# The last stages of a seven-block layer stack on one core: X kept in a reflected channel basis, trees routed from X, and the residual of the recurrence added by VectorE

## What is computed

```
x = x + _L1_attn_a_ref(_layernorm(x), ...)   # attention in segments of 64 tokens
x = x + _L1_ffn_ref(_layernorm(x), ...)      # soft decision tree, call 0
x = x + _L1_attn_b_ref(_layernorm(x), ...)   # linear recurrence (LRU)
x = x + _L1_ffn_ref(_layernorm(x), ...)      # the same tree, call 1

# tree:   gate = sigmoid(x @ Wq.T @ routers.T)              255 inner nodes
#         leaf_prob = product of gates along 8 levels        256 leaves
#         ret = leaf_prob @ leaf_values @ Wout_w.T + Wout_b
# LRU:    r, k, v = split(x @ W_rkv + b);  r = sigmoid(r);  k = exp(k)
#         u1 = scan(k * v), u2 = scan(k)   (decay lam per channel)
#         out = (u1 + g*k*v) / (u2 + g*k + 1e-6) * r  @ W_o + b_o
```

## Time and profile before

| what | value |
|---|---|
| time, median of 3 runs | 1137.93 us (1135.59 to 1144.2) |
| the profiled execution | 1128.02 us, span 1126.2 us |
| PE busy | 1003.1 us, 89% |
| DVE busy | 845.2 us, 75% |
| ACT busy | 748.8 us, 66% |
| POOL busy | 355.0 us, 32% |

### The profile page before, as it was taken

One profiled execution on the slowest core, in us unless ns is written; L12 is line 12 of the kernel. 1 busy time (PEld: TensorE's weight loads), 2 busy tenths in 40 slices (PEclk: granted clock), 3 DMA queues, 4 the chain that ended last, 5 costly groups with the idle time before them and its releaser, 6 DMA issues.

```text
span 1126.2 us, 20922 instructions
## 1 busy us (share of the span) xinstructions
PE 1003.1 (89%) x7682; PEld 622.6 (55%) x7682; DVE 845.2 (75%) x1518; ACT 748.8 (66%) x1235; POOL 355.0 (32%) x457
## 2 busy tenths in 40 slices
PE   7888899688867999899998999889898888898987
PEld 3333544387754444677653444676676775553355
DVE  4998887666654777777755776899999994768866
ACT  6895566345455447456777458687988776768885
POOL 1100057445553112000000114688878773000000
PEclk9999999899998999899999999799999998999999
DMA  7900055466641000000000000000000000000002
GB/s 189 294 0 1 1 150 160 145 200 212 220 145 66 1 0 11 2 2 2 1 2 1 0 1 10 1 3 2 3 2 3 16 3 10 1 1 1 0 1 76
DMA packets 42814, 54.53 MB, mean 48 GB/s; under 512 B 6251, under 2 KB 29372, under 8 KB 42716
## 3 DMA queue, kind: packets, MB, share of 16 engines
q1 hardware_dynamic: 38096, 42.75, 12.9%
q0 software_dynamic: 4288, 10.46, 2.5%
q10 hardware_dynamic: 332, 0.01, 0.0%
HBM read 22.11 MB, written 20.93 MB: 38 GB/s over the span
## 4 chain that ended last, share of the span: by engine, by line
PE 49%; DVE 22%; ACT 15%; issue 9%; POOL 2%; DMA 2%; SPq 0%; ACTq 0%; DVEq 0%
PE psum L88 4%; PE psum L1305 4%; PE psum L1277 3%; PE psum L954 3%; DVE arena L2510 3%; PE psum L1981 3%; DVE N L2519 3%; PE psum L1719 2%; DVE arena L2509 2%; PE psum L905 2%; PE psum L106 2%; ACT ln_std L115 2%; ACT ln_std L117 2%; PE psum L2326 2%; PE psum L918 2%
## 5 line engine op out<-in xcount | busy, mean ns | idle before, releaser
L2336 PE MATMUL psum<-ident,N 128*128 128x128 f32 x512 | 73.2, 288 | 18.4 <-POOL N L2479 17.8
L2425 ACT ACTIVATE N<-N 128x1024 f32<-128x1024 f32 x64 | 67.7, 1059 | 31.7 <-DVE N L2519 30.8
L2326 PEld LDWEIGHTS psum<-arena 32*128 32x128 f32 x1024 | 64.9, 194 | 25.7 <-issue 11.6
L88 PE MATMUL psum<-X,center 128*128 128x512 f32 x128 | 69.4, 631 | 10.6 <-DVE X L1062 4.2
L2326 PE MATMUL psum<-arena 32*128 32x128 f32 x1024 | 77.2, 293 | 1.6 <-ACT arena L2403 1.4
L768 POOL DMA_INDIRECT out_rows<-mixed,out_index x62 | 60.3, 972 | 57.1 <-DVE arena L844 32.0
L95 ACT ACTIVATE ln_sq<-psum 128x512 f32<-128x512 f32 x72 | 42.5, 591 | 52.2 <-PE psum L88 52.1
L2421 ACT ACTIVATE arena<-psum 128x1024 f32<-128x1024 f32 x64 | 65.7, 1026 | 16.9 <-PE psum L2336 16.7
L106 PE MATMUL psum<-ln_sq,mean 128*128 128x512 f32 x144 | 74.3, 607 | 2.1 <-ACT arena L151 1.1
L2336 PEld LDWEIGHTS psum<-ident,N 128*128 128x128 f32 x512 | 57.6, 146 | 28.1 <-POOL N L2479 22.9
L2479 POOL TENSOR_TENSOR N<-N,arena 128x512 f32<-128x512 f32 x64 | 67.8, 1059 | 0.0
(11 more groups left out here) (399 smaller groups left out, 2694.9 us busy)
## 6 DMA issues: line engine op xcount, KB each, us to landing
arena<-weights SPq DMA_DIRECT2D x31, 320.0 KB, 2.6
slot_rows<-zeros SPq DMA_DIRECT2D x1, 8060.0 KB, 26.6
arena<-slot_rows SPq DMA_DIRECT2D x31, 260.0 KB, 3.2
arena<-tw_rows SPq DMA_DIRECT2D x16, 256.0 KB, 3.6
arena<-out_rows SPq DMA_DIRECT2D x6, 512.0 KB, 5.0
out_dram<-arena SPq DMA_DIRECT2D x8, 256.0 KB, 2.8
arena<-in_L_attn_a_x_dram SPq DMA_DIRECT2D x3, 512.0 KB, 6.7
weights<-in_L_attn_a_eWk_dram SPq DMA_DIRECT2D x1, 1024.0 KB, 5.8
```

Source lines behind the costliest of these rows:

```text
L88: self.nc.tensor.matmul(k.bank[c % W][:], k.center[:], self.src(c), start=True, stop=True).then_inc(k.ln_centered, 1)
L2326: op = nc.tensor.matmul(scored[half][:, e * P:(e + 1) * P], k.sg_Q[b % 2][at, seg, 2 * j:2 * j + 2, :].rearrange("p h n -> p (h n)"), k.sg ...
L2336: op = nc.tensor.transpose(turned_to[:, e * P:(e + 1) * P], pr[n % 4][:, e * P:(e + 1) * P], k.ident[:])
L2425: nc.scalar.activation(pr[n % 4], pr[n % 4], ACT.Exp).then_inc(k.sg_exp, 1)
```

## The change

The reflection `k.house` is a symmetric orthogonal 128x128 matrix whose first row and column are 1/sqrt(128). In the basis that it makes, channel 0 holds the mean (times sqrt(128)), so that centring is only leaving channel 0 out.

- The norm before the segments (`TurningNorm`) multiplies by the reflection in place of the centring matrix, and DVE also copies the result back over X. From there on X stays reflected. All weights that read X or Y are multiplied by the reflection with row 0 cleared (`house_in`), and all that write to X by the reflection. This is done on PE and the weights are copied out of PSUM by DVE (for the segments' weights, in the norm) or by ACT (for the tree and the LRU, in iterations 52, 55, 56, 59 and 63 of the segments).
- The norms before both trees are gone. The trees route from X itself. Each token's 1/deviation is computed per token as a column (`RowMoments`: ACT squares a chunk, PE makes 4 products with one moving column, and ACT makes three small passes) and enters the sigmoids as their scale. So a chunk's gates are 8 sigmoids, 4 of 128x127 and 4 of 128x255, where there were 2 of 128x1024. For tree 0 these run inside the segments, for tree 1 at the LRU's end.
- The norm before the LRU (`TurnedNorm`) has no centring product. ACT squares X and DVE multiplies X.
- In the LRU the identity products are gone, and DVE adds X and the bias in the 8 instructions that write X. ACT's 8 such passes are gone.
- A tree's last level writes only the right children (512 numbers in place of 1024 per partition). The leaf values are differences for that half.
- The end turns X back with 4 products by the reflection per chunk, where there were 4 transposes.
- GpSimd builds the constants in the earlier `favor` block, and the LRU's weights are loaded with the tree's.

```diff
+class TurningNorm(Norm):
...
+        self.nc.tensor.matmul(k.bank[c % W][:], k.house, self.src(c), start=True, stop=True).then_inc(k.ln_centered, 1)
...
+    def scale(self, dve, c):
+        nc, k = self.nc, self.k
+        dve.wait_ge(k.ln_centered, self.centered0 + c + 1)
+        nc.vector.tensor_copy(self.src(c), k.bank[c % W][:]).then_inc(k.x_housed, 1)
+        dve.wait_ge(k.ln_rstd, self.n0 + c + 1)
+        nc.vector.tensor_tensor(self.dst(c), k.bank[c % W][:], k.ln_std[:, c % W, :], ALU.mult).then_inc(k.ln_out, 1)
+class TurnedNorm(TurningNorm):
...
+        self.nc.scalar.activation(self.k.ln_sq[:, c % W, :], self.src(c), ACT.Square).then_inc(self.k.ln_squared, 1)
...
+        nc.vector.tensor_tensor(self.dst(c), self.src(c), k.ln_std[:, c % W, :], ALU.mult).then_inc(k.ln_out, 1)
+class RowMoments:
...
+    def square(self, act, c):
+        k = self.k
+        if c >= 4:
+            act.wait_ge(k.tm_var, self.summed(c - 4))
+        self.nc.scalar.activation(self.squares[c % 4], k.X[:, c * CH:(c + 1) * CH], ACT.Square).then_inc(k.tm_sq, 1)
+
+    def sum(self, pe, c, to):
+        k = self.k
+        pe.wait_ge(k.tm_sq, self.summed(c))
+        for t in range(4):
+            op = self.nc.tensor.matmul(to[:, t:t + 1], self.squares[c % 4][:, t * P:(t + 1) * P], k.house_mean[:, 0:1], start=True, stop=True)
+        op.then_inc(k.tm_var, 1)
+
+    def deviation(self, act, first, end, source):
+        k, nc = self.k, self.nc
+        at, minus = (v[:, 4 * first:4 * end] for v in (self.rstd, self.minus))
+        k.tm_done += 1
+        act.wait_ge(k.tm_var, max(self.summed(c) for c in range(first, end)))
+        nc.scalar.activation(at, source, ACT.Ln, bias=k.eps[:, 0:1]).then_inc(k.tm_log, 1)
+        act.wait_ge(k.tm_log, k.tm_done)
+        nc.scalar.activation(at, at, ACT.Exp, scale=-0.5).then_inc(k.tm_rstd, 1)
+        act.wait_ge(k.tm_rstd, 2 * k.tm_done - 1)
...
-                nc.tensor.matmul(out_to[c][:], k.ident[:], k.X[:, at(b, c)], start=True, stop=False)
             if b == B - 2:
-                pe.wait_ge(k.lr_r, 2 * B)
+                pe.wait_ge(k.lr_k, 2 * B - 1)
+                pe.wait_ge(k.lr_kv, 2 * B - 1)
                 for c in range(4):
-                    pe.wait_ge(*(((k.lr_kv, 2 * B - 1), (k.lr_kv, 2 * B))[c < 2]))
-                    after.center(pe, c)
-                for c in range(2):
-                    after.variance(pe, c)
+                    moments.sum(pe, c, moment_at(c))
+            if b == B - 1:
+                for c in range(4, 6):
+                    moments.sum(pe, c, moment_at(c))
+                pe.wait_ge(k.lr_k, 2 * B)
+                pe.wait_ge(k.lr_kv, 2 * B)
+                tree_route(nc, k, pe, 1, 0)
             for c in range(2):
                 pe.wait_ge(k.lr_x, b + 1 if b + 1 < B else b + 1 + c)
-                nc.tensor.matmul(out_to[c][:], W_o, R[:, at(b, c)], start=False, stop=True).then_inc(k.lr_out, 1)
+                nc.tensor.matmul(out_to[c][:], W_o, R[:, at(b, c)], start=True, stop=True).then_inc(k.lr_out, 1)
 
         def project(b):
             for c in range(2):
...
-        def add(b):
+        def squares(b):
             for c in range(2):
-                act.wait_ge(k.lr_out, 2 * b + c + 1)
-                nc.scalar.activation(k.X[:, at(b, c)], out_to[c][:], ACT.Identity, bias=k.vec("lru_bo")).then_inc(k.lr_added, 1)
+                act.wait_ge(k.lr_added, 2 * b + c + 1)
+                moments.square(act, 2 * b + c)
 
...
-            if b == B - 1:
-                for c in range(4):
-                    after.square(act, c)
-                for c in range(2):
-                    after.deviation(act, c)
-            if b >= 1:
-                add(b - 1)
+            if b >= 2:
+                squares(b - 2)
+        squares(B - 2)
+        moments.deviation(act, 0, 4, k.bank[2][:, 0:16])
         over(B - 1)
-        add(B - 1)
+        moments.deviation(act, 4, 6, k.bank[3][:, 16:24])
+        squares(B - 1)
 
     @block.vector
...
+        def add(b):
+            for c in range(2):
+                dve.wait_ge(k.lr_out, 2 * b + c + 1)
+                nc.vector.scalar_tensor_tensor(k.X[:, at(b, c)], out_to[c][:], k.housed("lru_bo"), k.X[:, at(b, c)], ALU.add, ALU.add).then_inc(k.lr_added, 1)
...
             denominator(b)
+            if b >= 1:
+                add(b - 1)
             numerator(b)
         quotient(B - 1)
-
...
+def tree_route(nc, k, pe, call, n):
+    ready = (k.sg_x, k.lr_added)[call]
+    if call == 0 and n == 0:
+        pe.wait_ge(k.tw_copied, 7)
+    if n >= 2:
+        pe.wait_ge(k.tr_g, call * NCH + n - 1)
+    pe.wait_ge(ready, n + 1)
+    for t in range(4):
+        op = nc.tensor.matmul(tree_nodes(k, n)[:, t, 0:2 * P - 1], k.X[:, n * CH + t * P:n * CH + (t + 1) * P], k.gates[:, 0:2 * P - 1], start=True, stop=True)
+    op.then_inc(k.tr_z, 1)
...
-        op = nc.tensor.transpose(to[:, t, :], k.X[:, q * CH + t * P:q * CH + (t + 1) * P], k.ident[:])
+        op = nc.tensor.matmul(to[:, t, :], k.X[:, q * CH + t * P:q * CH + (t + 1) * P], k.house, start=True, stop=True)
...
+        for c in late:
+            moments.sum(pe, c, k.bank[2][:, 4 * c:4 * c + 4])
+        if call == 0:
+            pe.wait_ge(k.sg_ov, B * L // CH)
+            pe.wait_ge(k.sg_x, NCH)
+        else:
+            pe.wait_ge(k.lr_added, NCH)
+        tree_route(nc, k, pe, call, 1)
...
-            for s in range(2):
-                op = nc.scalar.activation(gates[n % 2][:, :, :, s], nodes[n % 2], ACT.Sigmoid, scale=(-1.0, 1.0)[s])
+            for t in range(TI):
+                at = slice(n * TI + t, n * TI + t + 1)
+                nc.scalar.activation(gates[n % 2][:, t, 0:P - 1, 0], nodes[n % 2][:, t, 0:P - 1], ACT.Sigmoid, scale=moments.minus[:, at])
+                op = nc.scalar.activation(gates[n % 2][:, t, 0:2 * P - 1, 1], nodes[n % 2][:, t, 0:2 * P - 1], ACT.Sigmoid, scale=moments.rstd[:, at])
...
+                if level == DEPTH - 1:
+                    nc.vector.tensor_tensor(lp[n % 2][1][:, :, 0:m], src, gates[n % 2][:, :, m - 1:2 * m - 1, 1], ALU.mult).then_inc(k.tr_lp, 1)
+                    continue
...
+    MOMENT = {25: 1, 28: 0, 41: 3, 44: 2, 57: 5, 60: 4, N + 1: 6}
+    SQUARE = {23: 1, 26: 0, 39: 3, 42: 2, 55: 5, 58: 4, N: 6}
+    WEIGHTS = {52: 0, 55: 1, 56: 2, 59: 3, 63: 4}
...
+            if n in MOMENT:
+                moment(n)
+            if n in WEIGHTS:
+                weights(n)
-            if n in (N + 2, N + 3):
+            if n == N + 3:
                 pe.wait_ge(k.sg_arg, N)
-                after.center(pe, n - N - 2)
+                tree_route(nc, k, pe, 0, 0)
...
+            if n in MOMENT:
+                moments.deviation(act, MOMENT[n], MOMENT[n] + 1, other[:, 0:4])
+            if n in WEIGHTS:
+                keep_tree_weights(nc, k, act, WEIGHTS[n], other)
+            if n in SQUARE:
+                act.wait_ge(k.sg_x, SQUARE[n] + 1)
+                moments.square(act, SQUARE[n])
+        act.wait_ge(k.sg_x, TURNS)
+        moments.square(act, TURNS - 1)
```

303 lines of the change are left out of this document (187 added, 116 removed).

## The result

The changed kernel is slower, not faster: median 1148.28 us (1139.25 to 1159.73, 20 runs) against 1138.28 (1131.03 to 1154.0, 20 runs) of the kernel before, ratio 1.0064, 95% interval 1.0041 to 1.0088. By the ratio that is +7.3 us, small (under the 1% of my forecast's bound) but clear of no change, where I forecast -10.9. The ratio compares fast runs alone (four runs of the changed kernel, at 1157 us and more, were in a slower state of the chip), while the medians take in all runs and so lie 10.0 us apart. The profiled execution has a span of 1148.2 us.

The account below looks back on a forecast made before the run. No engine is full overall; DVE is nearly full in segments and LRU, PE bounds a settled tree. 0.5+3-12.6-3.5-3.5+5.2 = -10.9, put on the median 1137.93, gave 1127.0 us; range 1119 to 1136.

Parts of the forecast that it names:

- the 1% of my forecast's bound: Whole kernel: about 1% (11.4 us) is what a measurement can tell from no change.
- Norm ahead, +0.5: Norm before the segments: ACT sets the pace, most added copies and products fit; +0.5 us (0 to 2).
- Insertions in the segments, +3: Sums and weight products added in the segments: most fit free PE and ACT time; +3 us (0 to 8).
- rival "slower": Segments: every insertion stalls as PE and ACT wait on bank 7; 22 us in place of 3, 1146; chance 0.05.
- Last output product to gate 0, -12.6: Segments' end to tree 0: short deviation work and table load replace the norm; -12.6 us (-13.5 to -11).
- Tree 0 and norm, -3.5: Tree 0 and the norm behind it: start +1.0, end -4.5; together -3.5 us (-5 to -1.5).
- the slow stretch that I had priced: Tree start: PE idles during gate 0, one 1.7 us route takes double length, of which 0.35 us shows.
- the rival of ACT as a tree's bound: Trees: ACT's gate and copy take 4.5 us per chunk, above PE's 4.32; total 1133; chance 0.12.
- LRU, -3.5: LRU: DVE's additions cost +2.8, the end gives -6.4, removed identity products worth nothing; -3.5 us (-5 to -1).
- PE's clock stays low: Thinned norm, LRU's end and both tree starts run at a low PE clock; +6 us, 1133; chance 0.10.
- Tree 1 and end, +5.2: Tree 1 and final turns: start +1.0, turn 6 +0.75, two-pass turns back +3.5; together +5.2 us (+4 to +8).
- my three signs of being wrong: Segments lose under 1 or over 8 us; tree turns over 4.5 apart; LRU's granted clock well below 0.96.

Follow-up runs that it names:

- e7_filler: Changed kernel with sums moved to iterations 31 and 47, plus the LRU's eight identity products back on PE, results unused: LRU 56.1 us, ratio 0.9912 to the kernel before.
- experiment 9: Changed kernel with sums moved from iterations 28 and 44 to 31 and 47, final turns as transposes, leaving out the reflection back: ratio 0.9916 to the kernel before.
- experiment 2: Changed kernel with the sums of chunks 0 and 2 moved from iterations 28 and 44 to 31 and 47: ratio 0.9901 to the kernel before.
- experiment 3: Changed kernel with two chunks' sums in one place (iterations 31, 47, 60) and one deviation for both: ratio 1.0063 to the kernel before, segments 248.0 us.

## Why the prediction was wrong

**Norm ahead, +0.5.** No run shows it or contradicts it; the spread of 701 to 720 us of the first exp buries it.

**Insertions in the segments, +3: this is the step that failed.** It went by free time per iteration ("PE has about 0.6 us free in each and ACT 0.8") and not by the place. 5.8 us is what the same work costs in good places, inside my 0 to 8. In iterations 28 and 44 the sums stand between a query projection and ACT's second read of it, and cost 13.9 us in iterations 29, 30, 45 and 46 (10.6 by the wait alone, with the slow clock behind it). Of the rest of the 21, some 5.4 us in iterations 26 to 28 are a slow stretch of this one profile (6.5 more, of which 1.1 is there in the good kernels too), and the others are the insertions' own cost less before's slow start. I had named this in the rival "slower" ("PE sits at bank 7 until ACT has read it"), priced it at 22 us and gave it 0.05, because "values and projections use the same bank in the same way". They don't: the order on both engines shows that only a query projection is read in two iterations, and that PE comes back to it after two, not one. For it to decide, two insertions were enough, not all seven.

**Last output product to gate 0, -12.6.** Right. From the last addition's start to gate 0 it was 17.87 us before and is 4.6 now, -13.3; the table's -14.0 counts from the last exp, where before had a short slow stretch (granted clock 0.67 and 0.65 from 936 to 946 us). The border after:

```profile
984.03 0.75 DVE L2712 SCALAR_TENSOR_TENSOR X<-psum,weights,X 128x512 f32<-128x512 f32 x1 [9.79 <-PE psum L2520]
985.50 1.05 PE L301 MATMUL psum<-weights,mixed 128*128 128x1 f32 x8 [1.50 <-ACT mixed L295]
987.34 1.28 ACT L46 ACT_TABLE_LOAD   x1
988.64 0.37 ACT L1877 ACTIVATE arena<-psum,weights 128x127 f32<-128x127 f32 x1
```

**Tree 0 and norm, -3.5.** Right to 0.1 us, with the slow stretch that I had priced (route 2 took 3.53 us): turn 1 came 9.91 us after gate 0, 8.91 before, the +1.0 of my sum. Turns stand 4.31 to 4.34 us apart, and gate 1 starts 2.43 us after gate 0, where I had 2.8 for a gate, so the rival of ACT as a tree's bound fell.

**LRU, -3.5: the second failure, measured +1.2.** The additions of sequences 0 and 1 cost what I said: the last gating is 41.3 us behind the norm, 38.4 before. What failed is "the removed identity products [...] were cover, worth nothing", and with it the end behind the last gating. With them gone PE's waits grew, and the granted clock up to the gating and behind it fell from 0.96 and 1.00 to 0.80 and 0.69. They are not all of it: with the eight products back and nothing made of them (e7_filler) it is 0.91 and 0.85. The next norm's centring, eight passes of 3.67 us, has gone too, with small sums in its place; what that does to the clock no run separates. Up to the gating the low clock cost nothing, since DVE sets the pace there; its price lies behind it. Two stretches of after (columns as in the earlier trace rows):

```profile
1041.40:1082.70 41.30, 32.54 (x81) 16.46 (x80) 41.07 (x33) 27.03 (x33) 0.00 (x0) 0.80 0.00 1
1082.70:1099.90 17.20, 15.43 (x56) 10.80 (x54) 6.79 (x9) 8.03 (x18) 0.00 (x0) 0.69 0.00 1
```

And its timeline from the sums of chunks 0 to 3 to the last addition:

```profile
1075.59 6.25 PE L301 MATMUL psum<-weights,mixed 128*128 128x1 f32 x32 [2.90 <-DVE arena L1526]
1089.75 3.75 PE L1795 MATMUL psum<-weights,X 128*128 128x255 f32 x8
1089.96 0.69 DVE L1696 TENSOR_TENSOR arena<-arena 128x512 f32<-128x512 f32 x1 [0.42 <-ACT arena L1631]
1093.29 1.96 PE L1585 MATMUL psum<-arena,weights 128*128 128x512 f32 x4
1094.43 1.61 DVE L1667 SCALAR_TENSOR_TENSOR X<-psum,weights,X 128x512 f32<-128x512 f32 x2 [3.78 <-PE psum L1585]
```

The last quotient came 7.25 us after the last gating (forecast 6.45), but its output products only at 1093.3, behind a route at half speed, and DVE waited 3.78 us. Gate 0 followed 17.2 us after the gating, forecast 12.5. Measured in two steps, the addition on DVE alone takes the LRU from 57.3 to 64.9 us (+7.6), and the rest of the change from there to 58.5 (-6.4), together +1.2. That my sum has a -6.4 as well is luck: there it was the end with DVE's additions and ACT's squares already in it, 12.5 in place of 18.9, and that end measured -1.7. My rival "PE's clock stays low" (0.10) was the true one here. The Trainium skill, "TensorE: Matmul & The Clock Gate", section "HAM oscillation — how this bites in real kernels", on which I had let that rival rest, spoke against the change, and I set it aside because before held 0.96 with a wait of 3.13 us in it; I should have asked what the clock is with those products gone.

**Tree 1 and end, +5.2.** Measured +2.8: 0.9 to turn 6 (forecast 1.75), and the turns back 1.9 in place of 3.5, since the last transfers had hidden room (experiment 9).

**The numbers.** With the insertions at 5.8 and the other terms as the table has them, the sum is 0.5+5.8-14.0-3.5+1.2+2.8 = -7.2; experiment 2 measured a ratio of 0.9901, -11.3 us of 1138.28 with 4.2 either way. So but for two places in a table the time would have come out as forecast, but in part by luck: the LRU would have been 4.7 us too long all the same, and the insertions 2.8, with the first border and tree 1 1.4 and 2.4 better than forecast against them. The range took in a bound of 8 us on the insertions; the bound itself was what was wrong. Two of my three signs of being wrong came: over 8 us lost in the segments, and a clock in the LRU well below 0.96.

**The better version** is the change with the sums at 31 and 47 and, in the LRU, PE's identity product and ACT's addition as before: 0.9892 (0.9852 to 0.9931) of the kernel before, some 12 us faster than it. Of these the moved sums are shown to count. The LRU's gain shows in its stretch (53.8 to 54.5 us in three profiles, 56.8 to 59.8 in the five without), 0.6 to 0.8 us of it comes back in tree 1 and the end (48.8 to 49.1 us, 48.3 in after), and what is left lies within the intervals of the whole.

## What to carry to other kernels

Free time per iteration says nothing about an insertion that shares a buffer: write down, for the iteration where it goes, who reads the buffer last and behind what on that engine. If that reader stands behind a step that needs this iteration's own products, the pipeline runs one iteration at a time. And where PE waits, its "hidden" products may be part of what keeps the rest at full clock: before removing them, look at the waits that they filled.

## What was new about the chip

PE's clock fell without a long wait: behind 16 one-column passes after 0.46 us of idle time (experiment 3), and in three of ten profiles of one and the same segments' code, which lost 4 to 8 us by it while the other seven lost 1 or nothing. The Trainium skill, "TensorE: Matmul & The Clock Gate", section "A second HAM failure mode: psum-queue depth-cycling", tells of such falls from short idle times between groups of products; these traces agree in that no long wait came ahead, and do not show that the short one was the cause. With eight products whose results nobody reads the LRU was shorter, by 4.45 us (62.9 to 58.45) in one pair of profiles and by 0.6 to 3.7 us in another order; they stand where PE otherwise waited 2.9 to 3.8 us ahead of the sums.
